# Moving the gating step of a state-space layer one slot later in the VectorE order

## What is computed

```python
# Mamba block, d_inner = 512, N = 16 states
h = rmsnorm(layernorm(x)) * norm_w
u, z = split(h @ in_proj_w.T)
uc = silu(causal_conv4(u) + conv_b)
dt, B, C = split(uc @ x_proj_w.T);  dt = softplus(dt @ dt_proj_w.T + b)
h_t = exp(dt * A) * h_{t-1} + dt * B * uc        # scan over time, for each of 16 states
y = sum_n h_t[n] * C[n] + uc * D
y = y * silu(z)
x = x + layernorm(y @ out_proj_w.T + layernorm(x))
# feed-forward, hidden 1024, ternary weights with scales
f = silu(xf @ w1) * (xf @ w2);  f = gelu(f @ h1);  f = gelu(f @ h2)
x = x + layernorm(f @ w3)
```

## Time and profile before

| what | value |
|---|---|
| median of 3 runs | 1822.44 us |
| lowest and highest run | 1806.45, 1822.51 us |
| the profiled execution: its time | 1806.45 us |
| the profiled execution: span of the core | 1804.6 us |
| mean granted TensorE clock in it | 0.887 of full |
| body 7 to body 8 to body 9, from the gating step to the next | 101.7 and 99.8 us |
| busy share: PE, DVE, ACT, POOL | 80%, 72%, 69%, 64% |
| DMA | 35 GB/s mean, 1 to 3 tenths busy |

### The profile page before, as it was taken

The page is one execution under the profiler, slowest core; times in us unless marked ns, Lnnn a source line. Parts: engine busy times, 40 slices in busy tenths (PEclk is TensorE's granted clock), DMA queues, the critical chain, the costliest instruction groups (busy, mean ns, idle before and its releaser), DMA issues.

```text
span 1804.6 us, 30656 instructions
## 1 busy us (share of the span) xinstructions
PE 1444.5 (80%) x9464; PEld 1276.7 (71%) x9464; DVE 1303.0 (72%) x1946; ACT 1236.5 (69%) x2638; POOL 1155.5 (64%) x1360
## 2 busy tenths in 40 slices
PE   4666688888888888888879888888888888887875
PEld 2122577787878787787778777787778877786875
DVE  2677887787778687787878787787778787886410
ACT  4454476868668775868768776868677777867543
POOL 1543656776677767676677766676677767677323
PEclk8687798899899888989998998999898998998987
DMA  3322100100101010100101010100101010101000
GB/s 109 105 91 76 36 26 20 37 26 25 39 26 39 24 38 27 37 25 21 44 24 39 26 41 24 37 26 26 38 26 43 20 44 20 36 26 31 2 8 7
DMA packets 38935, 63.78 MB, mean 35 GB/s; under 512 B 5216, under 2 KB 19424, under 8 KB 38640
## 3 DMA queue, kind: packets, MB, share of 16 engines
q10 hardware_dynamic: 18944, 33.83, 6.1%
q1 hardware_dynamic: 19696, 26.02, 4.5%
HBM read 55.38 MB, written 4.46 MB: 33 GB/s over the span
## 4 chain that ended last, share of the span: by engine, by line
PE 27%; ACT 20%; POOL 19%; issue 19%; DVE 14%; ACTq 1%; POOLq 1%; DVEq 0%; DMA 0%; SPq 0%
POOL S L471 11%; PE fP L618 8%; PE fP L619 7%; DVE S L1167 5%; ACT dA L880 4%; PE sT L642 4%; POOL Glo L541 4%; DVE acc L1181 3%; PE hP L606 3%; ACT Rw L1076 2%; ACT o L912 2%; PE fP L746 1%; ACT L1076 1%; DVE hP L1196 1%; PE fP L747 1%
## 5 line engine op out<-in xcount | busy, mean ns | idle before, releaser
L471 POOL TENSOR_TENSOR S<-X,Bs 128x1024 f32<-128x1024 f32 x256 | 611.8, 2390 | 344.2 <-PE sT L642 258.7
L1167 DVE TENSOR_TENSOR_SCAN S<-dA,S 128x512 f32<-128x512 f32 x512 | 620.8, 1214 | 166.5 <-POOL S L474 92.2
L880 ACT ACTIVATE dA<-delta,A 128x255 f32<-128x255 f32 x1024 | 446.3, 469 | 378.1 <-DVE S L1167 219.6
L618 PE MATMUL fP<-Ghi,w_h 128*128 128x256 f32 x2048 | 538.2, 300 | 56.4 <-DVE o L1241 46.5
L619 PE MATMUL fP<-Glo,w_h 128*128 128x256 f32 x2048 | 513.3, 288 | 0.0
L618 PEld LDWEIGHTS fP<-Ghi,w_h 128*128 128x128 f32 x2048 | 404.9, 198 | 64.7 <-DVE o L1241 49.9
L1181 DVE SCALAR_TENSOR_TENSOR acc<-sT,CT,acc 128x512 f32<-128x512 f32 x480 | 350.6, 733 | 111.3 <-PE sT L642 110.5
L619 PEld LDWEIGHTS fP<-Glo,w_h 128*128 128x128 f32 x2048 | 405.8, 198 | 0.4
L642 PE MATMUL sT<-ident,S 128*128 128x128 f32 x2048 | 337.7, 294 | 83.1 <-DVE acc L1181 68.1
L642 PEld LDWEIGHTS sT<-ident,S 128*128 128x128 f32 x2048 | 256.4, 151 | 143.6 <-DVE acc L1181 67.3
L541 POOL TENSOR_TENSOR Glo<-Rw,Ghi 128x1024 fp32r<-128x1024 f32 x96 | 225.9, 2356 | 127.1 <-ACT Ghi L1082 112.0
(11 more groups left out here) (133 smaller groups left out, 2032.0 us busy)
## 6 DMA issues: line engine op xcount, KB each, us to landing
Bs<-b_rows ACTq DMA_DIRECT2D x128, 256.0 KB, 3.2
Rw<-in_h SPq DMA_DIRECT2D x11, 512.0 KB, 3.2
xh<-in_x SPq DMA_DIRECT2D x16, 256.0 KB, 3.2
xt<-in_x SPq DMA_DIRECT2D x16, 256.0 KB, 4.0
out<-x SPq DMA_DIRECT2D x16, 256.0 KB, 2.8
x<-in_h SPq DMA_DIRECT2D x5, 512.0 KB, 3.2
Rw<-in_w SPq DMA_DIRECT2D x4, 512.0 KB, 4.6
w_in<-in_in_proj SPq DMA_DIRECT2D x1, 1024.0 KB, 5.4
```

The source lines that it names most:

```text
L471: pool.tensor_tensor(s[:, :, :], X[par][:, :, :], row[:, None, :].broadcast_to([P, DT, T]), ALU.mult).then_inc(scan_pool.sem, 1)
L618: pe.matmul(dst, w[:, i, cols_], hi[:, i, :], start=(j == 0), stop=False)
L880: a = act.activation(dA[half][:, i, 1:], delta[par][:, d, 1:], ACT.Exp, scale=A[:, d * N + n:d * N + n + 1])
L1167: a = dve.tensor_tensor_scan(pair, dA[half][:, :, :].rearrange("p d t -> p (d t)"), pair, 0.0, ALU.mult, ALU.add)
```

## The change

The gating step of the tail (four multiply-adds and two multiplies on VectorE, with their waits) moves from slot 1 to slot 2 of the body. In slot 2 the scan half `d01_1` (`back`) comes before `tail_step`, so the six instructions and their waits now stand behind this scan half and ahead of scan half `d23_1` of slot 3. Nothing else moves; no instruction is added or removed, and the other engines' programs are the same.

```diff
             def tail_step(f, fp, hs, head):
-                if hs == 1:
+                if hs == 2:
                     for i in range(2):
                         dve.wait_ge(tail_pe.sem, tail_pe.at(f, f"yT{i}"))
                         for d in (2 * i, 2 * i + 1):
```

## The result

| | before | after |
|---|---|---|
| median of 20 runs | 1814.21 us | 1826.16 us |
| lowest and highest | 1804.43, 1822.51 us | 1819.24, 1831.55 us |
| profiled execution: time, span | 1806.45, 1804.6 us | 1827.3, 1825.5 us |
| ratio after to before | | 1.0066, 95% interval 1.0051 to 1.0082 |

The change makes the kernel 12 us slower, 0.7%: clear of the measurement, and inside the 1% that the prediction called "same". With 20 runs the median of before is 8 us lower than the 1822.44 us of the first three.

The account below looks back on a forecast made before the run. No engine was busy for more than 80% of the span, so a chain of waits was taken to bound the kernel. Seven odd bodies at 2.3 us and seven even at 0 gave 1822.4 + 16 = 1838 us, range 1810 to 1860.

Parts of the forecast that it names:

- Step 1: Slot 2, VectorE: the scan half waits 3.3 us for ScalarE's decay and starts when it does today; gap not filled.
- Steps 2 to 4: Body 7: gating 4.0 us late, TensorE idle 6.2 ahead of out, out to turn 8.2, second h2 product 3.45 late.
- step 3: TensorE, body 7: start of out to end of turn takes 8.2 us at low clock, 7.7 today; other bound 6.4.
- the clock rival: Clock doesn't come back ahead of second h2 product: odd bodies 3.45 us late, even 1.05; 32 us, 1854 us; chance 0.25.
- Steps 5 and 6: Body 7: second h2 product and turn take 2.57 us, not 4.14; `x1` on GpSimd is 2.3 us late.
- Body 8, price 0: Even bodies: 4 us of room swallow most of the delay; second h2 product 1.05 late, turn 0.35 early; price 0.
- 7 x 2.3 + 7 x 0: Whole kernel: seven odd bodies cost 2.3 us each, seven even ones 0, together 16 us.
- More room: Out at full clock (6.4 us): odd bodies cost 0.5 us, even 0; 4 us in all, 1826 us; chance 0.18.
- Gap filled: Scan half runs in VectorE's wait for the transposes; 15.7 us of idle time come back, 1806 us or less; chance 0.12.

Follow-up runs that it names:

- after_early_odd: Changed kernel with ScalarE making the scan half's decay in slot 31 of the body before, for odd bodies alone; ratio 1.0005 to the kernel before.
- gate_waits: Kernel before (gating in slot 1, ahead of the scan half), but gating first waits for ScalarE's decay as the scan half does; ratio 0.9994.
- after_warm_out: Changed kernel with dummy matmuls on TensorE ahead of the wait for gating, 20 in odd and 14 in even bodies; ratio 0.9987 to the kernel before.
- before_warm_h2: Kernel before with dummy matmuls on TensorE ahead of the second h2 product's wait, 10 in odd and 16 in even bodies; ratio 0.9968.
- after_early_decay: Changed kernel with the scan half's decay made in slot 31 of the body before, in all bodies; it and its old-order twin measured 1.0156 and 1.0169.

## Why the prediction came out as it did

- *Step 1 (the scan half waits for the decay, the gap isn't filled)* held: 3.41 and 3.36 us of waiting for dA, where 3.3 was forecast. after_early_odd shows that without this wait in odd bodies the cost is gone; gate_waits shows that the wait alone doesn't make it. In body 8 the decay is late for another reason than in body 7: ScalarE itself waits 3.22 us for GpSimd ahead of it.
- *Steps 2 to 4* held: gating 4.0 late, idle time ahead of out 6.14 (6.2), out to turn 8.5 (8.2), second h2 product 3.7 late (3.45). That out's clock is a large part of it (8.2 against 6.4 us) was in step 3; in after_warm_out out takes 3.7 us instead of 5.9, and `x1` of odd bodies comes 2.3 us earlier. The rule of the Trainium skill, page "TensorE: Matmul & The Clock Gate", section "HAM oscillation — how this bites in real kernels", which was weighed there, fits out: 0.59 of 2.4 GHz behind 6.14 us of idle time. The prediction read a slow h2 product into it as well, if the short wait counts; the case that this section of the Trainium skill tells has longer waits than that, so it gives no ground for this. The trace shows 1.00 behind 1.44 us of idle time in bodies 2 to 15 of the changed kernel, so the clock rival fell.
- *Steps 5 and 6* held in body 7: product and turn 2.59 (2.57), `x1` 2.4 late (2.3), held by GpSimd.
- *Body 8, price 0*, held in direction: `x1` 0.4 early. The turn took 7.6 us from the start of out, not 8.2, so the o add was 0.3 late and not 1.05.
- *The sum was off in size, 16 against 12, and that it came so near is in part luck: errors cancel.* The step is "7 x 2.3 + 7 x 0": it prices all bodies by bodies 7 and 8. Bodies like 7 cost more than 2.3: the odd bodies 7 to 13 are 3.4 us longer, body 15 too. Body 14 was priced at 0, although rows 8 and 9 had its second h2 product at full clock, so that nothing could come back: it pays 2.3. Against that, in bodies 3 to 6 of the same profile the kernel before ran that product at 1.2 GHz throughout, `x1` of its odd ones came at 22.3 and of its even ones at 24.6, and over these four bodies together the change costs 0.6 us only. Between the two profiles the difference is 21 us, between the medians 12. The profiled execution of before was near the lower end of the runs (1806.45 of 1804.43 to 1822.51). The likely reason is that it had few bodies of the slower kind: in the second group the four executions above 1819 us have a mean granted clock of 0.877 or 0.878, the five under 1806 us 0.881 to 0.892. Only one execution was profiled, so this isn't shown. before_warm_h2 estimates the clock at the h2 product at 6 us.
- *Not foreseen:* the 1.0 us that body 7 loses behind slot 20, where a low clock falls on other matmuls once the body has shifted. I had followed the chain for 20 us only.
- *The base* was 8 us high: 1822.44 was the median of three runs, 1814.21 that of twenty. That moved the forecast of 1838 away from 1826, but not its difference.
- *Rivals.* Clock doesn't come back: fell. More room (out at full clock): fell for the change, and is what after_warm_out made true. Gap filled: fell, the decay comes when it did; and where the gap is filled (after_early_odd) the time is no lower than before.

## What to carry to other kernels

Before moving work behind an instruction "to fill a gap", find when that instruction's own inputs are ready: a scan that waits 3.4 us for another engine doesn't fill a 0.5 us gap, it holds what is queued behind it. Price the stage at TensorE's clock on both sides: what a longer wait ahead of one group of matmuls costs (out, 5.9 us instead of 4.8) can in part come back at the next group, if the wait ahead of that one shrinks (2.6 instead of 4.3). A few dummy matmuls in a wait that couldn't be avoided gave back 14 us here, about what the new place of the VectorE work cost. Price the change in several bodies of the loop, of both halves, and in the bodies behind the loop, and place the profiled execution among the runs first: here one kernel's runs lay 18 us apart.

## What was new on the hardware

- The clock at the second h2 product, over all traces: wherever the idle time ahead of it was 1.44 us, product and turn ran at 1.00 and took 2.6 us. Where it was 2.4 to 5.3 us they ran at 0.50 to 0.73 on average and took 3.4 to 4.6 us. In between both were seen: 1.00 behind 2.03 us (before_warm_h2, body 7) and 0.59 behind 2.14 us (after_early_decay, body 10).
- The idle time just ahead doesn't settle it everywhere. In the kernel before, out ran at 0.62 in body 10 behind only 1.38 us of it, and at 1.00 in body 3 behind 2.15. In body 10 the clock had fallen ahead of out: 1.00 from 1090 to 1092 us, 0.72 from 1092 to 1094 and 0.50 from 1094 on. From 1088 to 1094 TensorE was busy for 0.8 to 0.9 us in each 2 us, and no single pause in them was longer than 1.63 us.
- 128-column dummy matmuls of 4.6 us in total, with 1.5 us of idle time left behind them, kept out at 1.00 (3.7 us). TensorE's busy time went up, from 1440 to 1481 us, and the kernel's time down, by 14 us against the changed kernel.
- The effect has a tail: with a shift of 2.4 us in body 7, other matmuls 60 us later ran at 0.61 instead of 1.00, and the body lost another 1.0 us there; in body 8 a low stretch left that place and another appeared 20 us earlier.
